# A third place for feature rows in two sum passes of a graph kernel on one core

## The chip, the core and the metric

The program runs on one core of a Trainium2 chip. A core has a matrix engine (PE, with its weight loads shown apart as PEld), a vector engine (DVE), a scalar engine (ACT), GpSimd (POOL), a sequencer that only issues transfers (SP), and 16 DMA engines that all queues share. The metric is the device time of one launch in microseconds, as the median of several runs.

## What is computed

The reference runs two graph layers over 12,500 nodes with 64 features and 200,000 edges, each with a residual and a layer norm. Cut to what matters here:

```
def _demo_layer(h, src, dst, deg_pos, inv_deg, Wg, Wl, Ws, b):
    g = h @ Wg
    neigh_mean = segment_sum(h[dst], src) * inv_deg[:, None]
    extra = neigh_mean @ Wl + h @ Ws
    return elu(g + deg_pos[:, None] * extra + b)
x = _layernorm(x + three _demo_layers of x)
...
# second layer: per node i, over all edges in both directions and a self loop
seg_sum       = segment_sum([x[i], src_time], node_i)
neighbors_sum = relu(segment_sum([x[j], edge_feature, edge_time] @ W1.T + b1, node_i))
x = _layernorm(x + [neighbors_sum, seg_sum / count] @ W2.T + b2)
```

Two kinds of sums over edges appear. The first takes node vectors through the edges (three times in the first layer, once in the second). The second adds up the edges' own features, edge_attr_64 and its two siblings, per node. The second kind doesn't depend on any layer, so the kernel may do it whenever an engine has time.

## The kernel before

**Data.** The edges are sorted into chunks of K = 4 edges of one node tile; 128 chunks, one a partition, make a block, and there are NB = 544 blocks. A table in HBM called `by_src` holds, for each edge slot, a row of ROW = 196 floats (three features of 64, a one, and numbers). A block of it is 128 partitions by 4 x 196 floats, 392 KB: the feature rows of one *feature group*.

**Passes.** After the table is built, the passes follow one another: `wide_by_dst`, `wide_by_src`, then for each of the layers a `layer`, a `spread` (node vectors are picked out by one-hot products and written to `gathered`) and a `sums` (they are gathered back in the order of the source nodes and added up). The two sum passes that the change touches are `sums(sum2)` and `sums(sum3)`. The third one runs as `joint`, the last one as `sums(sum5)`.

**A turn of a sum pass.** `Sum` is the planner of a pass. A pass has NI = 34 turns of 16 blocks in four groups g of four. In a turn, POOL issues 16 indirect gathers (L720) into the 16 places of `ring`; SP loads the one-hots `ones` for a group into `oht_g` (L572, 256 KB each, four a turn); PE adds a block up with four products on each (L905, in `chunk_sum`), a block e of a group being 4 matmuls; DVE reduces (L1561) and adds to `node` (L1684). POOL may gather a group's four blocks again only after PE has done the same group of the turn before, and only after ACT has copied the indices (L1106).

**Feature groups in the pass.** At six marks of a turn, `((0, 3), (1, 1), (1, 3), (2, 3), (3, 1), (3, 3))`, given as (group, block), PE also does a feature group: `feature_sum` (L830, four f32 matmuls, eight records). Called m0 to m5 here. So m0 stands behind group 0, m1 in the middle of group 1, m2 behind it, m3 behind group 2, m4 in the middle of group 3 and m5 behind it. Each needs its rows in `frows`, which has two places (`frows[:, m % 2]`), its one-hots in f32, which ACT makes from `oh_s` into a part of `hring` (L1234, after the feature product before it, since there is one such place), and a bank of three that DVE must have added to `node` (L1651). `sum5` has four marks a turn, the other passes none.

**The order on SP.** SP issues its transfers in program order. For each group g of a turn (`features`, `body`): wait until PE has done the group's sums (L579), issue `ones` for the next turn's group; then for each mark of the group: wait until PE has done that feature product (L585), and fetch the rows two feature groups on into the place that came free (L569). The fetch behind m1 thus stands behind the wait for the end of group 1, and the fetch behind m4 behind the end of group 3.

**What lies idle in a sum pass.** `oh_s` has four places, of which the passes use 0 and 1; `hring` has 768 floats a partition, of which the f32 one-hots take 512.

Of the kernel before, what the change touches and what calls it, by code (L numbers as in the profile page):

```python
# [10 lines left out]
F32 = mybir.dt.float32  # L11
# [4 lines left out]
P = 128  # L16
# [11 lines left out]
K = 4  # L28
# [5 lines left out]
NI = NB // TURN  # L34
# [15 lines left out]
EF, ET, STF, ONE, LS, LD, ROW = 0, D, 2 * D, 3 * D, 3 * D + 1, 3 * D + 2, 3 * D + 4  # L50
FEAT = ONE + 1
# [20 lines left out]
def build(nc, x, src, dst, ef, stf, et, Wg1, Wl1, Ws1, b1, Wg2, Wl2, Ws2, b2, Wgo, Wlo, Wso, bo,  # L72
          W1t, c1, W2t, c2, out):
    with ExitStack() as ctx:
# [3 lines left out]
        def sb(name, shape, dt=F32):  # L78
            return ctx.enter_context(nc.sbuf_tensor(name, shape, dt))
# [4 lines left out]
        def sb_middle(name, shape, dt=F32):  # L84
            return middle.enter_context(nc.sbuf_tensor(name, shape, dt))

        def sem(name):
            return ctx.enter_context(nc.semaphore(name))
# [15 lines left out]
        ps = ctx.enter_context(nc.psum_tensor("ps", [P, 8, 512], F32))  # L104
# [21 lines left out]
        hring = sb("hring", [P, 8, HW], BF16)  # L126
# [63 lines left out]
        rows = sb_middle("rows", [P, 8, K, ROW])  # L190
        oh = sb_middle("oh", [P, 4, P, K], BF16)
        ohf = sb_middle("ohf", [P, 2, K, P])
# [7 lines left out]
        oh_s = sb("oh_s", [P, 4, P, K], BF16)  # L200
        ring1 = sb("ring1", [P, TURN, G1W], BF16)
        ring = ring1[:, :, :].rearrange("p s w -> p (s w)")[:, 0:TURN * GW].rearrange("p (s w) -> p s w", w=GW)
        frows = sb("frows", [P, 2, K, ROW])

        def four_one_hots(ap):
# [10 lines left out]
            frows[:, :, :, :].rearrange("p u k w -> p (u k w)").bitcast(BF16)[:, 2 * GW:4 * GW],  # L216
            oh_s[:, :, :, :].rearrange("p b n k -> p (b n k)")[:, 0:2 * GW],
            layers[:, :].bitcast(BF16)[:, 0:2 * GW])]
        fohf = hring[:, :, :].rearrange("p s w -> p (s w)").bitcast(F32)[:, 0:K * P].rearrange("p (k n) -> p k n", n=P)
        flat = ring1[:, :, :].rearrange("p s w -> p (s w)").bitcast(F32)  # L220
        flat_o = oht_g[:, :, :].rearrange("p b s -> p (b s)").bitcast(F32)
# [105 lines left out]
        joint_load = [sem(f"joint_load{s}") for s in range(2)]  # L327
        joint_ones = [sem(f"joint_ones{s}") for s in range(2)]
        joint_out = [sem(f"joint_out{s}") for s in range(4)]
        feat_row = [sem(f"feat_row{s}") for s in range(2)]  # L330
        feat_oh = sem("feat_oh")
        feat_ohf = sem("feat_ohf")
        feat_mm = sem("feat_mm")
        feat_add = sem("feat_add")

        class Sum:
# [3 lines left out]
            def __init__(self, number, k):  # L340
                self.k, self.q0, self.n0, self.i0 = k, number * NQ, number * NB, number * NI
                self.t0, self.g0 = number * NQ, (number + 2) * NI
                self.marks = ((0, 3), (1, 1), (1, 3), (2, 3), (3, 1), (3, 3)) if number < 2 else tuple((g, 3) for g in range(4))
                self.per = len(self.marks)
                self.f0 = number * 6 * NI if number < 2 else NB - 4 * NI
                self.banks = 3 if self.per == 6 else 4
                self.ones = sum_ones
                self.idx, self.got, self.oh = sum_idx, sum_got, sum_oh
                self.mm, self.red, self.add = sum_mm, sum_red, sum_add
# [65 lines left out]
        def _(sp):  # L415
# [14 lines left out]
            clears = table_chunks.rearrange("(b p) w -> p b w", p=P)  # L430
# [135 lines left out]

            def features(q):
                def fetch(f, u):
                    sp.dma_start(frows[:, u, :, :].rearrange("p k w -> p (k w)"), clears[:, f, :]).then_inc(feat_row[u], 16)  # L569

                def ones(j, g):
                    sp.dma_start(together(oht_g[:, 4 * g:4 * g + 4, :]), blocks(ones_d, 4 * j, 4, SL // 2)).then_inc(  # L572
                        q.ones[g], 16)

                def body(i, last):
                    for g in range(4):
                        if q.k == 1 and not last:
                            sp.wait_ge(q.mm, 4 * i + (q.t0 + g + 1))
                            sp.nop(nofuse=True)  # L579
                            ones(4 * i + (g + 4), g)  # L580
                        for m, (at, _) in enumerate(q.marks):
                            if at == g and not (last and m + 2 >= q.per):
                                f = q.per * i + (q.f0 + m)
                                sp.wait_ge(feat_mm, f + 1)
                                sp.nop(nofuse=True)  # L585
                                fetch(f + 2, m % 2)
                for u in range(2):
                    fetch(q.f0 + u, u)
                if q.k == 1:
                    sp.wait_ge(spread_mm, q.n0 + NB)  # L590
                    for g in range(4):
                        ones(g, g)
                with sp.Fori(0, NI - 1) as i:
                    body(i, False)
                body(NI - 1, True)
# [136 lines left out]
        def _(pe):  # L732
            flat = ps[:, :, :].rearrange("p b c -> p (b c)")
            pe.wait_ge(s_const, 1)
            for n in range(2):
                pe.wait_ge(s_keyf, n + 1)
                for g in range(KEYG):
                    mm = pe.transpose(flat[:, n * 2048 + g * P:n * 2048 + (g + 1) * P], keys_f[:, g, :], ident[:, :])
# [21 lines left out]
            for k in (1, 2):  # L760
                mm = pe.matmul(ps[0:T, 1 + k, 0:1], upper[0:T, 0:T], col[k][0:T, 1:2], start=True, stop=True)
            mm.then_inc(s_prep_t, 1)
            pe.wait_ge(s_prep_v, 3)
            for k in (1, 2):
                mm = pe.transpose(ps[0:T, 3 + k, 0:T], base[k][0:T, 0:T], ident[0:T, 0:T])
# [3 lines left out]
            for k in (1, 2):  # L769
                if k == 2:  # L770
                    pe.wait_ge(s_prep_v, 5)
                for a in range(2):
# [3 lines left out]
                    mm = pe.matmul(ps[0:1, 6 + a, 0:HB], iota_part[0:T, :], member[k][0:T, cut], start=True, stop=True)  # L776
# [50 lines left out]

            def feature_sum(bank, one_hots, rows_of):
                for k in range(K):
                    mm = pe.matmul(ps[:, bank, 0:FEAT], one_hots[:, k, :], rows_of[:, k, 0:FEAT], start=k == 0,  # L830
                                   stop=k == K - 1)
                return mm

            def wide_by_dst(q):
                def body(i, first, last=False):
                    for c in range(TURN):
                        b, u = TURN * i + c, c % 2
                        if not (last and c == TURN - 1):
                            pe.wait_ge(q.oh, b + 2)
                            if not first or c > 0:  # L840
                                pe.wait_ge(q.oht, b)
                            turned(3 - u, oh[:, (c + 1) % 4])
                        pe.wait_ge(q.ohf, b + 1)
                        if not first or c > 1:
                            pe.wait_ge(q.add, b - 1)
                        feature_sum(u, ohf[:, u], rows[:, c % 8])
                        pe.wait_ge(q.oht, b + 1)
                        pe.wait_ge(q.hc, b + 1)
                        if not first or c > 1:
                            pe.wait_ge(q.g, b - 1)  # L850
                            pe.wait_ge(q.gv, b - 1)
                        pe.nop(nofuse=True)
                        pick(4 + 2 * u, oht[:, c % 8, :], hring[:, c % 8, :]).then_inc(q.mm, 1)
                pe.wait_ge(q.oh, 1)
                turned(2, oh[:, 0]).then_inc(q.tr, 1)
                body(0, True)
                with pe.Fori(1, NI - 1) as i:
                    body(i, False)
                body(NI - 1, False, True)
# [76 lines left out]
            def sums(q):  # L936
                def body(i, first):
                    for g in range(4):
                        t, u = 4 * i + (q.t0 + g), g % 2
                        if q.k == 1:  # L940
                            pe.wait_ge(q.ones[g], 16 * i + (16 * q.i0 + 16))
                        else:
                            pe.wait_ge(q.oh, 4 * i + (g + 1))
                        for e in range(4):
                            pe.wait_ge(q.got[4 * g + e], 16 * i + (16 * q.g0 + 16))
                        if q.t0 > 0 or not first or g > 1:
                            pe.wait_ge(q.red, t - 1)
                        pe.nop(nofuse=True)
                        for e in range(4):
                            mm = chunk_sum(g, u, e, eight(oht_g[:, 4 * g + e, :]) if q.k == 1 else None)  # L950
                            if e == 3:
                                mm.then_inc(q.mm, 1)
                            for m, mark in enumerate(q.marks):
                                if mark == (g, e):
                                    f = q.per * i + (q.f0 + m)
                                    pe.wait_ge(feat_ohf, f + 1)
                                    pe.wait_ge(feat_row[m % 2], q.per * 8 * i + (8 * q.f0 + (m // 2 * 16 + 16)))
                                    if q.f0 > 0 or not first or m >= q.banks:
                                        pe.wait_ge(feat_add, f - (q.banks - 1))
                                    feature_sum(4 + m % q.banks, fohf, frows[:, m % 2]).then_inc(feat_mm, 1)  # L960
                loop(pe, body)

            def layer(q):
# [980 lines left out]
```

## Time and profile before

| | us |
|---|---|
| median of 3 runs | 9617.37 (9608.22 to 9624.15) |
| profiled execution, its own time | 9606.42 |
| its span | 9604.6 |
| `sums(sum2)`, first gather to last feature product | 5097.6 to 5892 |
| `sums(sum3)`, first to last reduce on DVE | 6376.7 to 7164.0 |
| `sums(sum5)`, from first to last one-hot product | 8591.9 to 9359.8 |

Over the span PE is busy 69%, DVE 62%, POOL 50%, ACT 39%, and the DMA engines moved 256 GB/s on average. These are means over stages with different limits: what a change of the sum passes is worth has to be read from windows inside these passes. Both passes have the same shape: a long even part, and at the end a part of some 120 us where the moved GB/s falls from about 300 to about 200 while the DMA engines stay busy.

### The profile page before, as it was taken

Reading aid. Unit: us, or ns where it says so; the run is one execution under the profiler, and the core shown is the slowest. Engines: PE = TensorE matmul, PEld = TensorE weight load, DVE = VectorE, ACT = ScalarE, POOL = GpSimd, SP = SyncE. Lnnn points to the kernel's source line nnn. Section 1 sums busy time; section 2 is a strip of 40 time slices with the busy share of each in tenths; the row PEclk is TensorE's granted clock in tenths of the full one; section 3 lists DMA queues with packets and bytes.
Section 4 is the critical chain, followed back from the end, with each engine's and each line's share of the span. In section 5 each row is a group of like instructions: output and inputs, shape, how many; then the busy total and the mean of one; then the engine's idle time right before and its main releaser. Section 6 shows DMA issues by size and latency. Waiting matters only on the chain.

```text
span 9604.6 us, 193424 instructions
## 1 busy us (share of the span) xinstructions
PE 6594.0 (69%) x46642; PEld 5845.8 (61%) x46642; DVE 5951.8 (62%) x16064; ACT 3698.9 (39%) x9003; POOL 4757.6 (50%) x4833
## 2 busy tenths in 40 slices
PE   7899999940079998655566675657664566656667
PEld 6788889940079997555445665446653455545556
DVE  8899997520076665554775445854448756546657
ACT  0011110000068887776593112951126954431111
POOL 0027777777734444776005662036640056647760
PEclk5555555555589999777799997999987988878876
DMA  9988887666589998878499994998974999987770
GB/s 383 391 279 199 199 198 179 157 157 158 149 273 326 332 331 283 239 237 215 146 396 315 302 301 106 394 342 294 302 197 158 393 353 352 353 237 218 213 188 14
DMA packets 1665463, 2463.57 MB, mean 256 GB/s; under 512 B 985413, under 2 KB 1057081, under 8 KB 1665385
## 3 DMA queue, kind: packets, MB, share of 16 engines
q1 hardware_dynamic: 1325672, 1499.58, 46.0%
q0 software_dynamic: 292608, 911.36, 32.7%
q10 hardware_dynamic: 47104, 51.75, 2.5%
q8 instruction: 30, 0.49, 0.0%
q14 instruction: 49, 0.39, 0.0%
HBM read 1435.51 MB, written 1022.63 MB: 256 GB/s over the span
## 4 chain that ended last, share of the span: by engine, by line
DMA 24%; PE 22%; issue 16%; DVE 14%; POOL 13%; ACT 7%; ACTq 2%; DVEq 2%; SPq 1%; POOLq 0%
PE ps L830 10%; DMA frows<-by_src 10%; POOL by_src L645 9%; DMA oht_g<-ones 4%; DMA ring<-gathered,gidx 4%; PE ps L823 3%; PE ps L905 3%; DMA rows<-by_src,gidx 2%; DMA gathered<-ring 2%; ACT ring L1204 2%; DVE mask L1484 2%; POOL ring L720 2%; POOL ring L700 2%; DVE ohj L1393 2%; DVE prod L1471 2%
## 5 line engine op out<-in xcount | busy, mean ns | idle before, releaser
L720 POOL DMA_INDIRECT ring<-gathered,gidx x2176 | 2130.3, 979 | 2634.6 <-DMA gathered<-ring 1584.4
L645 POOL DMA_INDIRECT by_src<-prow,ppos x1562 | 1524.2, 976 | 1108.7 <-DMA ppos<-pos 636.2
L823 PE MATMUL ps<-hring,oht_g 128*128 128x192 bf16 x8704 | 1031.7, 257 | 659.5 <-DMA oht_g<-oht 255.4
L1561 DVE TENSOR_REDUCE red<-ps 128x256 f32<-128x768 f32 x680 | 649.4, 955 | 1108.3 <-PE ps L905 934.9
L830 PE MATMUL ps<-frows,hring 128*128 128x193 f32 x4352 | 954.1, 368 | 533.4 <-DMA frows<-by_src 335.8
L823 PEld LDWEIGHTS ps<-hring,oht_g 128*128 128x128 fp8e4 x8704 | 713.6, 101 | 905.7 <-issue 867.7
L830 PEld LDWEIGHTS ps<-frows,hring 128*128 128x128 f32 x4352 | 799.1, 213 | 616.6 <-issue 412.7
L905 PE MATMUL ps<-ring,oht_g 128*128 128x192 bf16 x7616 | 921.0, 270 | 257.7 <-DMA ring<-gathered,gidx 122.5
L1639 DVE CAST ring<-ps 128x384 bf16<-128x384 f32 x1632 | 838.8, 553 | 254.8 <-PE ps L823 220.0
L788 PE MATMUL ps<-snap,oht_e 98*128 98x98 f32 x3130 | 956.0, 445 | 0.0
L905 PEld LDWEIGHTS ps<-ring,oht_g 128*128 128x128 fp8e4 (+1 forms) x7616 | 735.8, 109 | 350.8 <-issue 312.8
L788 PEld LDWEIGHTS ps<-snap,oht_e 98*128 98x128 f32 x3130 | 854.6, 333 | 17.9
L1204 ACT CAST ring<-ps 128x384 bf16<-128x384 f32 x1632 | 849.1, 521 | 8.2 <-PE ps L823 8.2
L830 PE MATMUL ps<-rows,ohf 128*128 128x193 f32 x4352 | 835.3, 335 | 21.9 <-ACT ohf L1115 21.3
L1106 ACT COPY gidx<-move 128x4 int32 (+1 forms) x816 | 156.3, 194 | 1788.5 <-DVE node L1544 1124.5
L679 POOL DMA_INDIRECT rows<-by_src,gidx x544 | 520.0, 956 | 631.9 <-ACT loc L1111 477.5
L1234 ACT CAST hring<-oh_s 128x512 f32<-128x512 bf16 x408 | 267.6, 656 | 1252.5 <-PE ps L830 1245.4
L830 PEld LDWEIGHTS ps<-rows,ohf 128*128 128x128 f32 x4352 | 698.0, 190 | 30.9 <-ACT ohf L1115 27.0
L1090 ACT COPY snap<-ps 98x490 f32<-98x490 f32 x313 | 177.7, 568 | 1345.2 <-PE ps L790 515.0
L700 POOL DMA_INDIRECT ring<-gathered,gidx x544 | 581.4, 1069 | 213.4 <-issue 160.6
L818 PE MATMUL ps<-ident_bf,oh 128*128 128x128 bf16 x2176 | 212.4, 220 | 654.8 <-DVE oh L1548 654.7
L1214 ACT COPY hring<-node 128x192 bf16 x1632 | 641.8, 394 | 40.3 <-issue 38.5
(240 smaller groups left out, 12635.4 us busy)
## 6 DMA issues: line engine op xcount, KB each, us to landing
gathered<-ring SPq DMA_DIRECT2D x408, 768.0 KB, 5.8
by_src<-zeros SPq DMA_DIRECT2D x34, 6272.0 KB, 46.6
frows<-by_src SPq DMA_DIRECT2D x544, 392.0 KB
oht_g<-oht SPq DMA_DIRECT2D x544, 256.0 KB, 5.9
gathered<-got SPq DMA_DIRECT2D x136, 776.0 KB, 6.2
oht_g<-ones SPq DMA_DIRECT2D x408, 256.0 KB
prow<-in_edge_attr_n SPq DMA_DIRECT2D x284, 352.0 KB
gathered<-frows SPq DMA_DIRECT2D x136, 384.0 KB
```

The source lines that it names most:

```text
L645: pool.indirect_dma_start(out=table, out_offset=bass.IndirectOffsetOnAxis(ap=ppos[:, s, j:j + 1], axis=0), in_=prow[:, s, j, :], in_offset ...
L679: pool.indirect_dma_start(out=rows[:, c % 8, :, :].rearrange("p k w -> p (k w)"), out_offset=None, in_=table_chunks, in_offset=offsets(g, ...
L700: pool.indirect_dma_start(out=ring1[:, c, :], out_offset=None, in_=gb1, in_offset=offsets(g, c % 4)).then_inc(q.got[c], 16)
L720: pool.indirect_dma_start(out=ring[:, c, :], out_offset=None, in_=rows_of, in_offset=offsets(g, c % 4)).then_inc(q.got[c], 16)
L788: pe.matmul(where, oht_e[0:T, v, l * P:(l + 1) * P], snap[0:T, v, l * T:(l + 1) * T], start=True, stop=False, skip_group_check=True)
L823: mm = pe.matmul(ps[:, bank + k // 2, k % 2 * HW:(k % 2 + 1) * HW], eight(one_hots)[:, k * P:(k + 1) * P], parts, start=True, stop=True, s ...
L830: mm = pe.matmul(ps[:, bank, 0:FEAT], one_hots[:, k, :], rows_of[:, k, 0:FEAT], start=k == 0, stop=k == K - 1)
L905: mm = pe.matmul(ps[:, 2 * u + e // 2, e % 2 * 256:e % 2 * 256 + HW], oh_sum[u][:, e, :, k] if one_hots is None else one_hots[:, k * P:(k ...
L1204: act.copy(ring[:, c, 0:2 * HW], ps[:, 2 * (c % 4), 0:2 * HW]).then_inc(q.g, 1)
L1214: act.copy(hring[:, e, :], parts_at(at[e])).then_inc(q.hc, 1)
L1561: return dve.tensor_reduce(red[:, u, :, 0:D], sums_of(bank)[:, :, 0:HW].rearrange("p b (a d) -> p b d a", d=D), AX.X, ALU.add)
L1639: dve.tensor_copy(ring[:, c, 2 * HW:4 * HW], ps[:, 2 * (c % 4) + 1, 0:2 * HW]).then_inc(q.gv, 1)
```

## The change

A third place for the rows of feature groups is added for the passes with six groups a turn (`sum2`, `sum3`). It isn't one piece of memory: the rows of k = 0 and 1 lie in places 2 and 3 of `oh_s`, those of k = 2 in the rest of `hring`, and those of k = 3 in a new tile `frow_3`. The groups go round the three places (m % 3), SP fetches the rows three groups on, and the third place's fetch is three transfers (196 KB, 98 KB and 98 KB) where it was one of 392 KB. That is 2 of the 6 fetches of a turn. Its semaphore rises by 48 for each group. The first fetch into the third place stands behind the wait for the end of the spread pass, since `hring` is in use until then. `sum5` keeps two places.

```
+        frow_3 = sb("frow_3", [P, ROW])
+        third = [oh_s[:, 2:4, :, :].rearrange("p b n k -> p (b n k)").bitcast(F32)[:, 0:2 * ROW],
+                 hring[:, :, :].rearrange("p s w -> p (s w)").bitcast(F32)[:, K * P:K * P + ROW], frow_3[:, :]]
+        third_k = [third[0][:, 0:ROW], third[0][:, ROW:2 * ROW], third[1], third[2]]
+        fslots = [[frows[:, u, k, :] for k in range(K)] for u in range(2)] + [third_k]
...
-        feat_row = [sem(f"feat_row{s}") for s in range(2)]
+        feat_row = [sem(f"feat_row{s}") for s in range(3)]
...
+                self.slots = 3 if self.per == 6 else 2
+                self.row0 = 2 * NI * min(number, 2)
...
                 def fetch(f, u):
-                    sp.dma_start(frows[:, u, :, :].rearrange("p k w -> p (k w)"), clears[:, f, :]).then_inc(feat_row[u], 16)
+                    if u < 2:
+                        sp.dma_start(frows[:, u, :, :].rearrange("p k w -> p (k w)"), clears[:, f, :]).then_inc(
+                            feat_row[u], 16)
+                    else:
+                        sp.dma_start(third[0], clears[:, f, 0:2 * ROW]).then_inc(feat_row[2], 16)
+                        sp.dma_start(third[1], clears[:, f, 2 * ROW:3 * ROW]).then_inc(feat_row[2], 16)
+                        sp.dma_start(third[2], clears[:, f, 3 * ROW:4 * ROW]).then_inc(feat_row[2], 16)
...
-                            if at == g and not (last and m + 2 >= q.per):
+                            if at == g and not (last and m + q.slots >= q.per):
                                 f = q.per * i + (q.f0 + m)
                                 sp.wait_ge(feat_mm, f + 1)
                                 sp.nop(nofuse=True)
-                                fetch(f + 2, m % 2)
+                                fetch(f + q.slots, m % q.slots)
...
+                    fetch(q.f0 + 2, 2)
...
-                                    pe.wait_ge(feat_row[m % 2], q.per * 8 * i + (8 * q.f0 + (m // 2 * 16 + 16)))
+                                    landed = 48 if m % q.slots == 2 else 16
+                                    pe.wait_ge(feat_row[m % q.slots],
+                                               2 * landed * i + landed * (q.row0 + (m // q.slots + 1)))
...
-                                    feature_sum(4 + m % q.banks, fohf, frows[:, m % 2]).then_inc(feat_mm, 1)
+                                    feature_sum(4 + m % q.banks, fohf, fslots[m % q.slots]).then_inc(feat_mm, 1)
```

On SP, in the loop over the turns of `sum2`, behind the sums of group 1 (m1 and m2), before:

```order
L572 DMA oht_g<-ones 128x1024
L569 ISA [waits feat_mm]
L569 DMA frows<-by_src 128x784
L569 ISA [waits feat_mm]
L569 DMA frows<-by_src 128x784
```

and of the change, at the same place:

```order
L585 DMA oht_g<-ones 128x1024
L597 REGISTER_ALU
L577 ISA [waits feat_mm]
L577 DMA frows<-by_src 128x784
L580 ISA [waits feat_mm]
L580 DMA oh_s<-by_src 128x392
L581 ISA
L581 DMA hring<-by_src 128x196
L582 ISA
L582 DMA frow<-by_src 128x196
```

The order of the waits is kept; the fetch behind m2 has become three transfers, with the setting of an address ahead of each.

On PE, in the same turn, the two feature products of group 1 (L905 and L919 are the one-hot sums), before:

```order
L959 REGISTER_ALU [waits feat_row1,feat_ohf]
L830 MATMUL ps<-frows,hring 128x193 [waits feat_add]
L830 MATMUL ps<-frows,hring 128x193 x3
L905 MATMUL ps<-ring,oht_g 128x192 x8
L956 REGISTER_ALU
L957 REGISTER_ALU [waits feat_ohf]
L830 MATMUL ps<-frows,hring 128x193 [waits feat_add,feat_row0]
L830 MATMUL ps<-frows,hring 128x193 x3
```

and of the change:

```order
L975 REGISTER_ALU [waits feat_row1,feat_ohf]
L844 MATMUL ps<-frows,hring 128x193 [waits feat_add]
L844 MATMUL ps<-frows,hring 128x193 x3
L919 MATMUL ps<-ring,oht_g 128x192 x8
L970 REGISTER_ALU
L972 ISA [waits feat_ohf]
L844 MATMUL ps<-oh_s,hring 128x193 [waits feat_add,feat_row2]
L844 MATMUL ps<-oh_s,hring 128x193
L844 MATMUL ps<-hring 128x193
L844 MATMUL ps<-frow,hring 128x193
```

No product is added or moved; m2 reads the third place and waits for its semaphore, where it waited for the place that m0 had used.

## Rows read from the trace of the kernel before

**Rows 1.** Windows of sum2, sum3, sum5, joint and sum2's end (columns in the first line).

```profile
core 0: us, PE busy (x) PEld busy (x) DVE busy (x) ACT busy (x) POOL busy (x), PEclk, DMA share, GB/s
5120.00:5740.00 620.00, 431.21 (x3166) 384.21 (x3163) 306.09 (x902) 122.24 (x283) 433.50 (x457) 0.97 0.91 302
6400.00:7020.00 620.00, 425.25 (x3136) 378.98 (x3136) 302.82 (x895) 121.59 (x281) 431.97 (x453) 0.97 0.91 299
8640.00:9260.00 620.00, 401.70 (x2712) 367.31 (x2712) 397.89 (x905) 94.26 (x226) 482.24 (x453) 0.84 0.72 216
7760.00:8400.00 640.00, 402.50 (x3424) 339.60 (x3422) 384.02 (x965) 315.67 (x964) 411.21 (x435) 0.83 0.99 353
5780.00:5870.00 90.00, 54.72 (x296) 48.94 (x296) 29.08 (x86) 11.44 (x26) 39.17 (x42) 0.75 0.94 198
```

**Rows 2.** Waits in 5120 to 5740: line, releaser, total us, times, longest.

```profile
PE ps L830 <- DMA frows<-by_src: 101.8, 88, 2.7
PE ps L830 <- issue: 73.5, 46, 2.8
PEld ps L830 <- DMA frows<-by_src: 64.9, 51, 2.8
```

**Rows 3.** Chain that ended last, 5110 to 5800, by line.

```profile
by line: DMA frows<-by_src 55.4%; PE ps L830 26.1%; PE ps L905 6.9%; issue 6.8%; SPq L572 1.6%; ACT hring L1234 1.1%; SPq L569 0.8%; DVEq L398 0.3%; DVE node L1684 0.2%; SPq L585 0.2%; DVE node L1651 0.2%; DVE oh_s L1548 0.2%; DVEq L1684 0.
```

**Rows 4.** SP's issues in order of time: start, us, line, transfer.

```profile
5402.74 0.33 SPq L572 DMA_DIRECT2D oht_g<-ones  x1
5403.31 0.33 SPq L569 DMA_DIRECT2D frows<-by_src  x1
...
5405.81 0.33 SPq L569 DMA_DIRECT2D frows<-by_src  x1
...
5409.88 0.33 SPq L569 DMA_DIRECT2D frows<-by_src  x1
```

**Rows 5.** PE in order of time, the same stretch: m1 to m5.

```profile
5400.26 1.57 PE L830 MATMUL ps<-frows,hring 128*128 128x193 f32 x8 [0.67 <-DMA frows<-by_src]
5401.67 0.82 PE L905 MATMUL ps<-ring,oht_g 128*128 128x192 bf16 x8
5404.01 1.57 PE L830 MATMUL ps<-frows,hring 128*128 128x193 f32 x8 [1.52 <-DMA frows<-by_src]
5405.42 1.48 PE L905 MATMUL ps<-ring,oht_g 128*128 128x192 bf16 x16
5408.12 1.54 PE L830 MATMUL ps<-frows,hring 128*128 128x193 f32 x8 [1.21 <-issue]
5409.50 0.82 PE L905 MATMUL ps<-ring,oht_g 128*128 128x192 bf16 x8
5410.64 1.56 PE L830 MATMUL ps<-frows,hring 128*128 128x193 f32 x8 [0.32 <-DMA frows<-by_src]
...
5415.14 2.27 PE L830 MATMUL ps<-frows,hring 128*128 128x193 f32 x7 [2.27 <-issue]
```

**Rows 6.** Groups by line, POOL's gathers: sum2's window, then sum5's (busy, mean ns, idle).

```profile
L720 POOL DMA_INDIRECT ring<-gathered,gidx x457 | 434.8, 951 | 186.8 <-issue 137.9 <-PE ps L905 48.0 <-ACT gidx L1106 0.9
...
L720 POOL DMA_INDIRECT ring<-gathered,gidx x453 | 484.5, 1070 | 138.1 <-issue 118.3 <-PE ps L905 12.2 <-ACT gidx L1106 7.6
```

**Rows 7.** DMA queues, 5120 to 5740: packets, MB, share of 16 engines.

```profile
q1 hardware_dynamic: 40556, 97.40, 46.5%
q0 software_dynamic: 29172, 89.62, 44.7%
```

**Rows 8.** DMA queue of SP in sum5's window, 8640 to 9260, and its issues.

```profile
q1 hardware_dynamic: 16241, 45.27, 21.6%
...
frows<-by_src SPq DMA_DIRECT2D x112, 392.0 KB
```

**Rows 9.** DMA queues of SP and ACT, 700 to 1300, and ACT's issues.

```profile
q1 hardware_dynamic: 247871, 46.90, 40.4%
q10 hardware_dynamic: 22323, 25.41, 21.4%
...
bc<-tidrow ACTq DMA_DIRECT2D x156, 160.0 KB
```

More of the change, by code:

```diff
@@ L829, in feature_sum @@
                 for k in range(K):
-                    mm = pe.matmul(ps[:, bank, 0:FEAT], one_hots[:, k, :], rows_of[:, k, 0:FEAT], start=k == 0,
+                    mm = pe.matmul(ps[:, bank, 0:FEAT], one_hots[:, k, :], rows_of[k][:, 0:FEAT], start=k == 0,
                                    stop=k == K - 1)
@@ L845, in body @@
                             pe.wait_ge(q.add, b - 1)
-                        feature_sum(u, ohf[:, u], rows[:, c % 8])
+                        feature_sum(u, ohf[:, u], [rows[:, c % 8, k] for k in range(K)])
                         pe.wait_ge(q.oht, b + 1)
```

## The prediction

> **What bounds the kernel now.** I first read the windows of the four sum stages, to see which engine is near its end in each; then who waits for whom in the even part of `sum2`; then the chain that ended last; and last one turn in order of time on PE and SP.
>
> The windows show that no engine is full in `sum2` and `sum3` [rows 1]: PE is busy 431 of 620 us, POOL 434, DVE 306, the DMA engines 91%. PE's clock isn't the matter (0.97 granted). POOL makes 457 gathers in 620 us, so a turn of 16 takes 620 / 457 x 16 = 21.7 us in `sum2`, and 620 / 453 x 16 = 21.9 us in `sum3`. PE's idle time lies ahead of the feature products: 101.8 us put down to the rows' transfer and 73.5 to nothing visible, in 28.6 turns, some 6 us a turn [rows 2]. The chain has the transfers of feature rows for 55% and the feature products for 26% of its length; gathers aren't in it at all [rows 3]. So the pass waits for fetch, product, fetch, product through the two places.
>
> One turn shows the loop. m1 starts at 5400.26 and takes 1.57. Its place is free at 5401.83, but SP issues the fetch at 5403.31, 1.48 later, since that stands behind group 1's sums and their `ones`. m3, which needs it, starts at 5408.12, 4.81 after the issue [rows 4, 5]. From m1 to m3 that is 7.86 us. m3's fetch leaves at 5409.88, 0.22 after its end, and m5 starts 5.26 later: m3 to m5 is 7.02. From m2 (5404.01, issue 5405.81) to m4 (5410.64) it is 6.63. A place serves three feature groups a turn, one of them with the late issue (m1 or m4): 7.9 + 7.0 + 6.6 = 21.5 us, which is the turn. Both places have the same sum. This loop, a latency, sets the pace.
>
> **What the change does to that loop.** Each place now serves two groups a turn. Place 0 has m0 and m3, both issued at once: 2 x 6.8 = 13.6 us. Place 1 has m1 and m4, both issued late: 2 x 7.9 = 15.8 us. Place 2 has m2 and m5, with three issues in a row, of which two more come before the last piece leaves: 2 x 0.33 us [rows 4] and the setting of two addresses, say 0.8 in all, so 2 x (6.8 + 0.8) = 15.2 us. All three lie under 20 us, so the waits of rows 2 for feature rows go, about 6 us a turn on PE. It isn't all gained: what is late next is POOL or the DMA engines.
>
> **POOL's floor.** In `sum5` POOL issues without a break: 484.5 busy and 138.1 idle make 622.6 for a window of 620, the gap being 138.1 / 453 = 0.305 us [rows 6]. In `sum2` a gather takes 0.951 us. Without waits that is (0.951 + 0.305) x 16 = 20.1 us a turn. `sum5` also shows that PE, ACT's indices and the 16 places of the ring let POOL run at its floor, where feature rows aren't late. I take the gather's 0.951 from `sum2` itself, since DVE's instructions there stay the same.
>
> **The DMA engines' floor.** Their share is 46.5 + 44.7 = 91.2% [rows 7], so a turn has 0.912 x 21.7 = 19.8 us of transfers. The bytes stay. What is added is pieces: a fetch has 16241 / 112 = 145 packets now [rows 8], and one into the third place three times that, 290 more. What a short packet costs beyond its bytes isn't shown for this transfer. Lower bound: nothing; below zero is excluded, since no byte is saved. Nearest row: SP's loads of 256-byte and shorter rows, 247,871 packets of 189 bytes on average at 40.4% of 16 x 600 us, 15.6 ns each [rows 9]; `sum5`'s fetches cost 0.216 x 16 x 620 = 2143 us for 45.27 MB, 47.3 ns a kB [rows 8], so 189 bytes would be 8.9 ns, and 6.7 are on top. 290 x 6.7 ns / 16 = 0.12 us a fetch, 0.24 a turn. Upper bound: ACT's loads of 1280-byte rows, 0.214 x 16 x 600 / 22323 = 92 ns a packet [rows 9]; 435 packets of 92 ns are 2.50 us of the 16 engines, against 2143 / 112 / 16 = 1.20 for a whole fetch, 1.3 more, 2.6 a turn. I take 0.24, because these loads come from the same queue and, like ours, each row from its own address, while ACT's read one HBM row 128 times. That gives 20.0 us at a full share; `joint` reaches a share of 0.99 [rows 1], for 20.2.
>
> **The turn.** Two limits of 20.1 and 20.2 us will not both be met to the end. At today's share of 0.91 nothing would be gained, at `joint`'s 0.99 all of it. I take 0.97, nearer to `joint`, as there too the transfers are always queued: 20.0 / 0.97 = 20.6 us.
>
> **Sum.** The even part lasts from 5105 to about 5765, 30.4 turns; `sum3` has as many. `sum2`: (21.7 - 20.6) x 30.4 = 33 us. `sum3`: (21.9 - 20.6) x 30.4 = 40 us. At the pass's end some 120 us go at 198 GB/s with the engines 94% busy, and POOL isn't the limit (42 gathers in 90 us) [rows 1]; a share of 0.98 would save 5 us, the pieces cost 1: 4 us a pass, 8 in all. Together 81 us. The extra address settings and issues lie on SP, which waits most of a turn, and cost nothing; without that cover they would be about 1.6 us a turn. The first fetch into the third place is first needed behind m1, after some ten gathers, and costs nothing. DVE's addition to `node` keeps its three banks. The profiled execution took 9606.4; less 81 that is 9525.4. The median stands 11 us above it (9617.4), so the forecast is 9536 us.
>
> Its own ends: at the floor of 20.1 us, (1.6 + 1.8) x 30.4 + 10 = 113 us, 9504. At a share of 0.945, 21.2 us a turn, (0.5 + 0.7) x 30.4 + 4 = 40 us, 9577.
>
> **Rivals.**
>
> *The transfers take longer as more of them are in flight.* Place 1 has the tightest loop: 2 x (1.57 + 1.48 + landing). With 4.8 us to land that is 15.7; 7.0 us make it 20.1, and 7.8 us today's 21.7. For it: the engines are 91% busy, and three fetches will queue where two did; ACT's copy and the late issue of m1 and m4 stay in the loop. Against it: 2.2 us of room. Landing in 7.5 us would give 21.1 us a turn and, with nothing at the ends, (0.6 + 0.8) x 30.4 = 43 us; in 7.7 us, 21.5 and 18 us. I put it at 9590.
> The Trainium skill (DMA: Bandwidth & Descriptors, section Latency and other measured facts) gives an HBM access 0.2 us on average and 2 us at high load. By that, landing could rise from 4.8 to 6.6 us, place 1's loop would take 19.3 us, and this rival would not bind; the trace of before has no second load level for the same fetch, so no run here shows it.
>
> *The mix is already at its limit.* If 0.91 is all that these short gathers and loads can reach together, the third place fills but the pace stays, and the pieces cost 0.24 x 68 = 16 us: 9633, no change by the measurement. Against it: `joint` moves 353 GB/s with the same gathers at 0.99, and `sum2` would need 302 x 21.7 / 20.6 = 318 [rows 1].
>
> *Small pieces cost engine time.* At the upper bound a turn has 19.8 + 2.6 = 22.4 us of transfers, at 0.99 22.6: (0.9 + 0.7) x 30.4 = 49 us more, and 2.6 x 8 turns at the two ends 21: 9617 + 70 = 9687. It decides the sign once a fetch in pieces costs over (0.99 x 21.8 - 19.8) / 2 = 0.9 us more than the 1.20 of a whole one.
> The Trainium skill speaks for this rival (DMA: Bandwidth & Descriptors, section Bandwidth): batch transfers to 1 MiB or more, it says, and its measurements fall from 341 GB/s at 1 MB to 138 at 64 KB. Our pieces of 98 KB lie near the low end. An estimate from those figures, 150 GB/s for each of two pieces and 200 for the one of 196 KB, is 2.3 us a fetch, 1.1 more than today's, and puts a turn at 22.2 us and the kernel near 9670. The trace disagrees so far: 392 KB land in 4.8 us but take 1.20 us of the engines, so most of a small transfer's time keeps no engine busy.
>
> **How the numbers follow.** Forecast 0.69; longer landing 0.15; already at the limit 0.10; costly pieces 0.06. A measurement of this kernel can tell about 0.2% from no change, 9598 to 9637. Faster: 0.69 and most of the second case, 0.81; same: the rest of it and the third, 0.12; slower 0.07. The range takes in the forecast's ends and the second case: 9500 to 9598.
>
> **What would show it.** In the profile after: over 5120 to 5740 about 620 / 20.6 x 16 = 480 gathers; POOL's idle near 0.33 us a gather; PE's waits for feature rows under 1 us a turn, and waits for gathers in `ring` in their place; a DMA share of 0.95 or more at 318 GB/s; SP's queue with some 290 more packets for each fetch in pieces, at about 7 ns each over its bytes. It is wrong if PE still waits at L844 for `frows` (the first rival), if the share stays at 0.91 with the feature waits gone (the second), or if the engines fill at 300 GB/s or less (the third). `spread`, `joint`, `sum5` and the layers should be as they were.

## The result and the profile after

The changed kernel takes 9501.87 us (median of 4 runs, 9477.91 to 9508.38), the kernel before beside it 9619.19. The ratio is 0.9875, with a 95% interval of 0.9859 to 0.9892: 1.25% less, some 118 us. 81 us were forecast. On the median of 9617.4 that the prediction started from, the ratio gives 9497, just outside its range of 9500 to 9598. The direction and the loop that the change opens were right, the size was too small by a third.

The changed kernel's profiled execution has a span of 9476.1 us, 128.5 less than before. The windows of its two sum passes, with the columns of [rows 1]:

```profile
core 0: us, PE busy (x) PEld busy (x) DVE busy (x) ACT busy (x) POOL busy (x), PEclk, DMA share, GB/s
5110.00:5690.00 580.00, 436.31 (x3204) 388.53 (x3203) 312.60 (x920) 130.06 (x287) 440.09 (x460) 0.96 0.96 326
6328.00:6908.00 580.00, 432.79 (x3195) 384.47 (x3194) 312.37 (x920) 130.51 (x285) 440.10 (x459) 0.96 0.96 326
```

460 gathers in 580 us are a turn of 580 / 460 x 16 = 20.17 us, 459 are 20.22, where before it was 21.7 and 21.9. (POOL may run up to 16 gathers ahead, so a turn counted by gathers is good to some 0.2 us. By DVE's reduces, 27 turns from the 5th to the 113th, it is 21.94 and 22.24 before, 20.27 and 20.27 after.) POOL's gathers in the first window (busy, mean ns, idle and its releasers; [rows 6] before):

```profile
L734 POOL DMA_INDIRECT ring<-gathered,gidx x460 | 440.7, 958 | 140.2 <-issue 128.0 <-ACT gidx L1122 7.0 <-PE ps L919 5.2
```

The idle time is 140.2 / 460 = 0.305 us a gather. That is the gap that `sum5` has, and 128.0 of the 140.2 us lie ahead of gathers that waited for nothing visible, so next to nothing holds POOL up any more; before it was 186.8 / 457 = 0.409. 0.958 + 0.305 us, 16 times, is 20.2 us: the turn.

What PE and ACT wait for in the same window (line, releaser, total us, times, longest; [rows 2] before), and the chain by line ([rows 3] before):

```profile
ACT gidx L1122 <- DMA ring<-gathered,gidx: 235.2, 88, 5.9
...
PE ps L919 <- DMA ring<-gathered,gidx: 84.2, 53, 4.0
...
PE ps L844 <- DVE node L1667: 23.1, 20, 2.9
...
PE ps L844 <- DMA frows<-by_src: 11.5, 8, 2.2
...
PEld ps L844 <- DMA frow<-by_src: 10.2, 15, 1.5
...
PE ps L844 <- DMA frow<-by_src: 5.4, 10, 1.2
```

```profile
by line: DMA ring<-gathered,gidx 24.2%; issue 21.6%; POOL ring L734 17.9%; PE ps L844 11.7%; DMA frows<-by_src 7.1%; PE ps L919 7.1%; DVEq L405 3.0%; DVE node L1700 2.1%; DVE node L1667 1.0%; DVE oh_s L1564 1.0%; DVEq L1700 0.7%; SPq L585 0
```

PE now waits for gathers ahead of the one-hot sums, and for feature rows 11.5 + 5.4 = 16.9 us where it was 101.8 (in 620 us). The transfers into `frows` had 55% of the chain and have 7% left; gathers and POOL, absent before, have 42%.

From the first reduce to the last, the passes take 5098.3 to 5829.5 and 6316.4 to 7044.6, 731.2 and 728.2 us. Before they took 783.0 and 787.3. That is 51.8 + 59.1 = 110.9 us. Of it, (21.7 - 20.17 + 21.9 - 20.22) x 30.4 = 98 us are in the even parts, which leaves 13 for the ends. By the reduces, 98 us are in the 27 turns named above, 9 in the last 23 reduces of the two passes (some 160 us each), and 4 at their starts. The rest of the 128.5 lies where the change does nothing: `joint`, from its first reduce to the first of `sum5`, took 868.0 us before and 860.0 after, and 870 to 882 in the seven kernels below that leave it as it is.

### The profile page after: what moved, and what is told of

The parts are those of the page before. It is cut to its first block, busy times and chain, and to the rows that moved or that the text cites. A ratio compares the mean times of both kernels' runs of the same rounds, so it can differ in the third digit from the quotient of the medians.

```text
span 9476.1 us, 194354 instructions
## 1 busy us (share of the span) xinstructions
PE 6529.7 (69%) x46642; PEld 5816.2 (61%) x46642; DVE 5940.9 (63%) x16064; ACT 3714.7 (39%) x9003; POOL 4755.1 (50%) x4833
## 4 chain that ended last, share of the span: by engine, by line
DMA 21%; PE 20%; issue 18%; POOL 16%; DVE 14%; ACT 7%; DVEq 2%; ACTq 1%; SPq 1%; POOLq 0%
POOL by_src L659 9%; PE ps L844 8%; DMA ring<-gathered,gidx 7%; POOL ring L734 5%; DMA oht_g<-ones 4%; PE ps L837 3%; DMA gathered<-ring 3%; PE ps L919 3%; ACT ring L1220 2%; POOL ring L714 2%; DMA rows<-by_src,gidx 2%; DVE mask L1500 2%; DMA frows<-by_src 2%; DVE ohj L1409 2%; ACT hring L1230 2%
## 5 line engine op out<-in xcount | busy, mean ns | idle before, releaser
L837 PE MATMUL ps<-hring,oht_g 128*128 128x192 bf16 x8704 | 997.6, 256 | 698.0 <-DMA oht_g<-oht 268.1
L919 PE MATMUL ps<-ring,oht_g 128*128 128x192 bf16 x7616 | 911.1, 268 | 446.4 <-DMA ring<-gathered,gidx 314.8
L919 PEld LDWEIGHTS ps<-ring,oht_g 128*128 128x128 fp8e4 (+1 forms) x7616 | 716.6, 108 | 566.4 <-issue 538.2
L844 PE MATMUL ps<-frows,hring 128*128 128x193 f32 x3264 | 720.2, 371 | 140.7 <-DMA frows<-by_src 85.6
L844 PEld LDWEIGHTS ps<-frows,hring 128*128 128x128 f32 x3264 | 614.3, 217 | 169.5 <-issue 71.1
L844 PEld LDWEIGHTS ps<-rows,ohf 128*128 128x128 f32 x4352 | 698.0, 190 | 25.1 <-ACT ohf L1131 21.7
L832 PEld LDWEIGHTS ps<-ident_bf,oh 128*128 128x128 bf16 x2176 | 163.4, 114 | 665.9 <-issue 653.3
```

Source lines behind the costliest of these rows:

```text
L837: mm = pe.matmul(ps[:, bank + k // 2, k % 2 * HW:(k % 2 + 1) * HW], eight(one_hots)[:, k * P:(k + 1) * P], parts, start=True, stop=True, s ...
L919: mm = pe.matmul(ps[:, 2 * u + e // 2, e % 2 * 256:e % 2 * 256 + HW], oh_sum[u][:, e, :, k] if one_hots is None else one_hots[:, k * P:(k ...
```

## The experiments

Theory A was that with two places a loop of landing and product sets the turn, and with three POOL does. Its rivals let the transfers' total, or the price of small pieces, set it. Times of runs are compared by ratios to the kernel before on the same chip. "Turn" below is 580 us x 16 over the gathers in that time, in the even part of `sum2` and of `sum3`.

| kernel | median us | before us | ratio | turn, us | DMA share |
|---|---|---|---|---|---|
| changed | 9501.9 | 9619.2 | 0.9875 | 20.17, 20.22 | 0.96 |
| two places, early fetch | 9596.4 | 9640.2 | 0.9955 | 21.14, 21.00 | 0.93 |
| three places, early fetch | 9536.7 | 9640.2 | 0.9881 | 20.17, 20.13 | 0.97 |
| three places, all in pieces | 9557.6 | 9640.2 | 0.9912 | 20.13, 20.17 | 0.99 |
| three places, half the bytes | 9510.2 | 9640.2 | 0.9860 | 20.17, 20.13 | 0.86 |
| two places, half the bytes | 9488.4 | 9615.0 | 0.9866 | 20.13, 20.17 | 0.85 |
| two places, in pieces | 9687.6 | 9615.0 | 1.0076 | 22.69, 22.63 | 0.91 |
| changed, again | 9497.6 | 9615.0 | 0.9884 | 20.13, 20.13 | 0.96 |
| three places, spread indices | 9255.9 | 9615.0 | 0.9625 | 20.09, 20.13 | 0.96 |
| the same, again | 9251.2 | 9618.8 | 0.9617 | 20.13, 20.13 | 0.95 |
| two places, spread indices, on a slower chip | 10927.5 | 11100.4 | 0.9829 | 27.29, 26.14 | 0.75 |
| two places, spread indices | 9351.6 | 9618.8 | 0.9722 | 21.24, 21.68 | 0.92 |

### Is it the loop? Fetches of half the bytes, in both kernels

```
# both, in the turns of sum2 and sum3
-  frows[:, u, :, :]  <- clears[:, f, :]
+  frows[:, u, 0:2, :] <- clears[:, f, 0:2 * ROW]
# third place: widths ROW, ROW // 2, ROW // 2 where they were 2 * ROW, ROW, ROW
```

The rest of the rows stays stale, so the feature sums are not the reference's. With three places:

> The changed kernel, but in the turns of the two passes each fetch brings only half of its bytes (k = 0 and 1, and half widths in the third place); the other half of the rows is left stale, so the feature sums are not those of the reference. This takes 3.6 us of transfers out of a turn. Theory A (POOL sets the turn): the even part stays at 20.1 to 20.2 us a turn, only the passes' ends get shorter, 9470 to 9500 in all. Rival B (the DMA engines set it): the turn goes to well under 20 us and the kernel below 9440.

With two places:

> The kernel before (two places), but in the turns of the two passes each fetch brings only k = 0 and 1 of the rows, half of its bytes; the rest is left stale, so the feature sums are not those of the reference. Theory A (landing time in a loop of fetch and product sets the pace with two places): a fetch of half the bytes lands 0.5 to 1.2 us earlier, three fetches make a place's loop, so a turn falls from 21.7 to the 20.2 of POOL or close above it: 9500 to 9530. Rival B (the transfers' total sets it): 3.6 us of 19.8 fewer, the turn would go to 20.2 as well, but the engines' share would stay near 0.9; under A it falls to 0.85 or less.

The windows of both, three places first:

```profile
5129.00:5709.00 580.00, 445.85 (x3210) 400.46 (x3209) 311.81 (x918) 130.90 (x287) 440.15 (x460) 0.93 0.86 267
```

```profile
5118.00:5698.00 580.00, 429.94 (x3216) 380.58 (x3216) 310.95 (x916) 132.95 (x288) 439.82 (x461) 0.98 0.85 268
```

With three places, 18% of the moved bytes taken away (326 to 267 GB/s at the same pace) don't change the turn at all: 460 gathers as before. So the changed kernel isn't bound by its transfers, though they keep the engines 96% busy. With two places, the same cut brings all of what the third place brings: 461 gathers. In the timelines of SP and PE in `sum2`, a product that waited for its rows starts 4.2 us after the fetch's issue on average (53 products), where it was 5.2 us (88 products) before. Since the full bytes fit as well once there is a third place, what that place bought is time to land. The second kernel's 9488 is below the 9500 that were expected, and as good as the changed kernel's 9498 on the same chip: its passes take 1456.6 us together, that one's 1462.4.

### Is it the loop? An earlier issue

```
-  if q.k == 1 and not last:      # wait for the group's sums, then its one-hots
-      ...
-  for m, (at, _) in enumerate(q.marks):
+  for early in (True, False):
+      if not early and q.k == 1 and not last:
+          ...
+      for m, (at, e) in enumerate(q.marks):
+          # only marks with (e < 3) == early
```

> The kernel before, two places, with one thing changed: SP issues the fetches behind m1 and m4 ahead of its wait for the group's sums and of the group's one-hots, so that no fetch is late. Theory A (the loop of fetch and product through the places sets the pace with two places, POOL's issue with three): a place's loop becomes 3 x 6.8 = 20.4 us a turn instead of 21.5, so the even parts save 1.1 to 1.4 us x 61 turns, 65 to 85 us: 9530 to 9555. Rival B (the mix of transfers is near its own limit, and the third place helps by keeping more in flight): the same bytes with no more in flight, no change, 9610 to 9620.

> The changed kernel with the same move on SP: the fetches behind m1 and m4 go out ahead of the group's wait. Theory A: POOL is at its floor of 20.2 us a turn and no fetch is late, so nothing changes: 9495 to 9510, a turn of 20.2. Rival C (the three places' own loop still costs something): the remaining waits for feature rows go, 5 to 15 us less.

With two places the turn falls by 0.6 and 0.9 us and the kernel by 0.45%, 43 us: the rival (no change) is out, but 20.4 us a turn was too low, and 9574 us on the scale of 9617 lies between what the two had expected. In the trace, the fetches issued at 5403.78 and 5410.82 reach their products late (the first row holds two fetches; the second of them left at 5406.84, for the product of m3):

```profile
5403.78 3.39 SPq L569 DMA_DIRECT2D frows<-by_src  x2
...
5410.82 0.33 SPq L569 DMA_DIRECT2D frows<-by_src  x1
```

```profile
5409.02 1.57 PE L831 MATMUL ps<-frows,hring 128*128 128x193 f32 x8 [1.74 <-DMA frows<-by_src]
...
5416.14 1.57 PE L831 MATMUL ps<-frows,hring 128*128 128x193 f32 x8 [1.37 <-DMA frows<-by_src]
```

5403.78 to 5409.02 is 5.24 us and 5410.82 to 5416.14 is 5.32, against the 4.8 to 5.3 of [rows 4, 5]. Three such in a loop, with a product of 1.57 and 0.22 to the issue, are 3 x 7.1 = 21.2 us, which is the turn. One turn is few fetches, so here are the averages over `sum2`'s windows, from the timelines of SP and PE (us; three rounds of a place are a turn, so the columns only split the turn into its parts):

| two places | end of product to next issue, three rounds | issue to the product served | the same, of products that waited for rows |
|---|---|---|---|
| before | 1.8 | 5.1 | 5.2 |
| early fetch | 0.5 | 5.3 | 5.35 |
| half the bytes | 1.8 | 4.5 | 4.2 |
| in pieces | 1.8 | 5.5 | 5.4 |
| spread indices | 1.8 | 5.0 | 5.0 |

The early issue takes 1.3 us out of a turn, as expected, and 3 x 0.2 come back in landing. The 20.4 us rested on one turn's landing times, with a mean of 5.0, where the average was 5.2. Whether the rest comes with the faster pace or from the chip (the kernel before takes 9640 there) wasn't separated. With three places the move changes nothing, as it must where POOL sets the turn: 0.9881 of 9617 is 9503, within the 9495 to 9510 expected.

### What do pieces cost?

```
+  for k, n in ((0, 2), (2, 1), (3, 1)):
+      sp.dma_start(frows[:, u, k:k + n, :]..., clears[:, f, k * ROW:(k + n) * ROW]).then_inc(feat_row[u], 16)
```

> The changed kernel with every fetch of feature rows in three transfers (also those of the first two places, and in the last sum pass): 4 more fetches a turn in pieces. Theory A (a piece costs the DMA engines nothing that is felt, POOL sets the turn): 9500 to 9512, a turn stays 20.2 to 20.3. Rival B (the engines are full at a share of 0.97 and pieces cost, 0.12 us a fetch as the prediction had it): 0.5 us a turn, 30 us: 9530; at the upper bound of the prediction, 1.3 us a fetch, 25 us a turn, 9800.

> The kernel before (two places) with every fetch of feature rows in three transfers. Here a fetch's landing time is in the loop that sets the turn. Theory A: the last piece leaves 0.8 us later and the pieces cost 0.12 us of the engines, three fetches are in a place's loop, so a turn gets up to 2.5 us longer if the last piece lands that much later, nothing if the pieces land together sooner: 9640 to 9790. Rival F (a fetch in pieces lands no later than a whole one, as its parts go side by side): 9615 to 9640.

SP's queue in `sum2` with three places, all fetches in pieces, and then the changed kernel's (packets, MB, share of the 16 engines over 580 us):

```profile
q1 hardware_dynamic: 91128, 99.44, 52.1%
```

```profile
q1 hardware_dynamic: 57581, 98.74, 49.5%
```

33,547 more packets take 2.6% of 16 x 580 us, 241 us. 33 of them are the 0.7 MB more, at the 47.3 ns a kB of [rows 8]; 208 / 33547 = 6.2 ns a packet. Set against the other profiles of kernels with three places, in both passes, it is 6.0 to 7.2. The prediction had 6.7, from other transfers. This is a price in busy share, not in time. The turn stays at 20.13 and 20.17 at a share of 0.99:

```profile
5129.00:5709.00 580.00, 442.74 (x3211) 395.57 (x3211) 311.61 (x918) 130.98 (x287) 439.68 (x461) 0.95 0.99 328
```

The kernel is still slower than the one with three places beside it, 9557.6 against 9536.7, so theory A had the turn right and the time wrong (9533 on the scale of 9617, against 9500 to 9512). The time matched the rival's 30 us, but not by the rival's mechanism, since the turn didn't move. The two profiles put the difference elsewhere: the passes take 736.5 and 745.4 us against 732.8 and 738.2, and `sum5` 777 against 766. Each is one profile, and `sum5` takes 759 to 770 us in the other runs without spread indices, and 770 with two places and pieces, so where the 21 us go is only hinted at.

With two places, in pieces, the window of `sum2` has 409 gathers:

```profile
5122.00:5702.00 580.00, 385.16 (x2817) 343.56 (x2816) 274.33 (x808) 108.41 (x251) 389.57 (x409) 0.96 0.91 288
```

Here the pieces are felt in the turn: 22.7 us, 1.0 and 0.7 more, and 73 us in all. Three fetches are in a loop, so the last piece lands some 0.3 us later, as the table above has it too. That is much less than the 1.05 us by which it leaves later (three issues take 1.38 us from the first's start to the last's end in this trace), and so neither the full delay nor none is what came; 9688 lies in the theory's range of 9640 to 9790.

### The slow ends

The ends gained little (9 to 13 us in two passes), and stayed at this (the changed kernel, `sum2`; 44 gathers in 100 us, columns as above):

```profile
5720.00:5820.00 100.00, 56.33 (x308) 50.02 (x306) 30.86 (x93) 12.11 (x26) 41.50 (x44) 0.73 0.95 192
```

The blocks there are the spare ones that the planner allots, and every empty chunk had the same index, so all partitions of such a gather read one row of zeros. The table has 128 rows of zeros, one for each partition, and 127 of them lay unused.

```
-  move[k] = min(movef, ZERO)
+  movef = min(movef - iota_part, ZERO)
+  move[k] = movef + iota_part
```

> The changed kernel with another change: the index of an empty chunk is ZERO + p for partition p where it was ZERO for all, so that the gathers of the last blocks of each pass read 128 different rows of zeros and not one row 128 times. Theory D (the slow end of each pass, at 200 GB/s with busy engines, is that one row): the ends run at the even part's pace, 25 us less in each of the two sum passes, and as much in the other four passes that gather, 100 to 180 us in all: 9330 to 9410 beside 9510 for the changed kernel. Rival E (the ends are slow for another reason, as fewer transfers in flight): no change.

100 us near the end of the same pass with this:

```profile
5600.00:5700.00 100.00, 75.77 (x558) 67.77 (x557) 54.42 (x160) 22.96 (x50) 75.94 (x80) 0.94 0.95 327
```

80 gathers instead of 44, at the even part's pace. The DMA queue of the gathers in the two windows, of the changed kernel first:

```profile
q0 software_dynamic: 3142, 9.64, 60.1%
```

```profile
q0 software_dynamic: 5043, 15.49, 45.5%
```

A gather has 64 packets (29,389 for 460 in the even part), so these are the packets of 49 and 79 gathers; 44 and 80 is what POOL issued meanwhile. 60.1% of 1600 us for 49 is 19.6 us of engine time each, 45.5% for 79 is 9.2. Reading one row 128 times made a gather 2.1 times as dear. The other transfers waited behind them: the median time to landing of `ones` in the two windows, with the indices on one row and spread:

```profile
oht_g<-ones SPq DMA_DIRECT2D x9, 256.0 KB, 18.9
```

```profile
oht_g<-ones SPq DMA_DIRECT2D x20, 256.0 KB, 5.0
```

This kernel takes 9255.9 us, ratio 0.9625 (0.9609 to 0.9641), 242 us under the changed kernel beside it; 100 to 180 were expected, 25 of them in each of the two sum passes. Between the two profiles of the set, 48 and 50 us are in `sum2` and `sum3`, 81 in `joint` and `sum5` together, 24 in `wide_by_src` and 12 in `wide_by_dst` (these two against the first profile of the changed kernel): 215 of 224.

Whether the third place and this add up:

> The kernel before (two places) with the indices of empty chunks spread over 128 rows, as in e7_pads_spread. If the third place and the spread indices act on different parts of a pass, each keeps its own gain: the even part stays at a turn of 21.7 to 21.9 us, the slow ends go, and the kernel takes 230 to 250 us less than before, 9365 to 9390. If the third place was needed for the ends (landing times there too), less: 9400 to 9450.

That set ran on a chip where the kernel before took 11100 us; its ratio of 0.9829 says nothing on the question, and a turn took 27.3 us there at a DMA share of only 0.75. The next expectation speaks of longer transfers there, which the trace doesn't bear out: the median landing of the loads from `oht` is 5.4 us there and 5.9 in the first profile of before, and 26 products that waited for their rows start 4.0 us after the issue on average. What it has instead are 173 us in `sum2`'s window in which ACT, ahead of its f32 one-hots, waits for a releaser that the profile can't place; before has none of this. The two kernels were run side by side again:

> The kernel of e10_two_pads again (two places, indices of empty chunks spread), since the set of e10 ran on a chip on which the kernel before took 11100 us and every transfer longer. Where the kernel before takes its 9617: the even parts stay at 21.7 to 21.9 us a turn, the slow ends go, 9365 to 9390, ratio 0.974 to 0.977. If the third place was needed for the ends, 0.978 or more.

> The kernel of e7_pads_spread again (three places, spread indices), beside e11 on one chip. If the two gains only add up, its ratio is e11's less 0.0115 to 0.013, near 0.9625.

```profile
5061.00:5641.00 580.00, 405.59 (x3013) 360.46 (x3012) 293.39 (x864) 116.52 (x270) 414.83 (x437) 0.98 0.92 308
```

```profile
5062.00:5642.00 580.00, 441.04 (x3206) 396.66 (x3207) 311.56 (x916) 130.40 (x287) 439.89 (x461) 0.94 0.95 327
```

With two places the ratio is 0.9722 (0.970 to 0.9743), with three 0.9617 (0.9597 to 0.9638), 0.0105 less where 0.0115 to 0.013 were expected. The third place is worth 100 us here and 118 without the spread indices, so they nearly add up. The passes say the same: 727.0 and 736.5 us with two places, 682.5 and 682.6 with three, 98 us where it was 111. With two places the kernel is faster than the 9365 to 9390 expected, because its even parts are: 21.24 and 21.68 us a turn where 21.7 to 21.9 was expected, with rows that land in 5.0 us instead of 5.2. By the reduces, the third place saves 85 us in the 27 even turns of the two passes, 98 without the spread indices; in the last 23 reduces it saves 16, and 9 without. So what is missing of the 111 us is missing in the even parts. The landing times are from one profile each, on two chips, so whether the spread indices shortened them isn't shown.

## Why the prediction was right or wrong

**What bounds the kernel: right.** The loop of two places was shown from both sides: landing made shorter (half the bytes) takes the two-place kernel to 20.15 us a turn, made longer (pieces) to 22.7, and an earlier issue to 21.1. The sum of 21.5 us that the prediction took from one turn is a little low: its three landings had a mean of 5.0 us, where the average over the window is 5.1, and the turn is 21.7 us by gathers and 21.9 by reduces.

**The loops with three places: right.** PE's waits for feature rows in the first window after are 11.5 + 5.4 = 16.9 us in 28.8 turns, 0.6 us a turn (the weight loads' 10.2 us come beside them), the "under 1 us a turn" of the prediction. 2.2 us of room in the tightest loop was enough.

**POOL's floor: right.** 20.1 us were worked out from 0.951 + 0.305; 20.17 and 20.22 came, from 0.958 + 0.305.

**The DMA engines' floor and the turn: wrong, and this is the step that failed.** The prediction counted the share as work (0.912 x 21.7 = 19.8 us a turn), put it near full at 20.0 us, and then took a share of 0.97 because two limits "will not both be met to the end": 20.6 us a turn. The step from two floors to a turn above both was argued from `joint`, not worked out. Measured, POOL's limit is met to the end, at shares of 0.86, 0.96, 0.97 and, with all fetches in pieces, 0.99. The difference, (20.6 - 20.17 + 20.6 - 20.22) x 30.4, is 25 of the 30 us that the sum was short in the passes; 5 more are the 13 us against 8 outside the even parts. The share isn't a fixed amount of work: it times the turn was 19.8 us before and 0.96 x 20.17 = 19.4 after, with the pieces added. A gather's engine time follows from the queue's share: 0.447 x 16 x 580 / 428 = 9.7 us in the kernel before, 0.469 x 9280 / 460 = 9.5 in the changed one, and 0.511 x 9280 / 461 = 10.3 where the engines have half the feature bytes. The less busy the engines were, the longer a gather's packets counted as busy; the mix of transfers differed with it. The trace of before had this already, in the gathers' queue in the windows of `sum5` and of `joint` of [rows 1] (packets, MB, share):

```profile
q0 software_dynamic: 28876, 88.77, 50.8%
```

```profile
q0 software_dynamic: 27778, 85.35, 40.1%
```

0.508 x 16 x 620 / 453 = 11.1 us a gather at a share of 0.72, and 0.401 x 16 x 640 / 435 = 9.4 at 0.99. The prediction didn't set the two side by side. The remaining 7 of the 37 us between 81 and 118 lie outside the two passes and within the interval of the ratio.

**The price of pieces: right** as a price in the engines' share, 0.24 us a turn was taken with 6.7 ns a packet, and 6.0 to 7.2 were measured. The upper bound from ACT's loads (1.3 us a fetch) was far off. At a turn set by POOL the price isn't felt in the turn. Where the loop sets it, pieces cost 0.7 to 1.0 us a turn for six fetches, by landing later.

**The ends: right in size**, 9 to 13 us where 8 were taken. But the prediction saw the 198 GB/s and didn't ask why. Spread indices brought 98 us in these two passes and 242 in all, twice the change's own gain. It had a sign of it at hand: it noted that ACT's loads, at 92 ns a packet, read one HBM row 128 times.

**Costs of the issues on SP: right** in that nothing of it shows: with three places, moving the fetches ahead of the group's wait leaves the turn where it is. The last piece leaves 1.05 us after the first, not 0.8; the room in the loop covered that too.

**The rivals.** Longer landing shows with two places at 21.1 us a turn (5.3 us on average where it was 5.1) and doesn't bind with three. A mix at its limit is excluded by the changed kernel itself, which moves 326 GB/s where 318 would have done. Costly pieces would have decided above 0.9 us a fetch; they cost 0.11 to 0.13, in engine time. (The 22.2 us a turn that the prediction set for small transfers would give (0.5 + 0.3) x 30.4 + 2.2 x 8 = 42 us, 9659 and not 9670.) The turn of 20.6 is most of what stood between the forecast and the result, and the range ended at POOL's floor, with only 10 us for the ends.

## What to carry to other kernels

Where transfers and products go round n places, add up one place's loop from issue to issue and set it against the turn; if it equals the turn, a place more is worth up to the distance to the next engine's floor, and here it was all of it, at a DMA share of 0.96. Average the landing times over a window, since one turn's can be off by several per cent. Don't take the share as work: test it by moving fewer bytes. And where GB/s fall while the share stays high, look at the addresses.

## What the hardware showed beyond that

- A gather of one and the same HBM row by 128 partitions cost 19.6 us of DMA engine time against 9.2 for 128 different rows (64 packets and 0.197 MB either way). The loads of `ones` beside them landed in 18.9 us instead of 5.0.
- A gather's engine time was lower at a higher share: on one chip 10.1 us at 0.86, 9.8 at 0.93, 9.5 at 0.97 and 0.99; on another 10.3 at 0.85, 9.6 at 0.91, 9.4 at 0.96. Chips differ by some 0.3 us (9.1 at 0.95 on a third). The share went together with the feature bytes and the pace, and which of them does it wasn't separated.
- Three transfers of 196, 98 and 98 KB in place of one of 392 KB cost 6 to 7 ns of engine time for each further packet, and the last one landed about 0.3 us later.
- One chip took 11100 us for the kernel that takes 9617 elsewhere, with a DMA share of 0.75 in `sum2`. Its cause stays open.
